# Squares streamed past a column of ones, and small operations on VectorE ahead of the steps

## The reference, cut to what matters

```
xn = layer_norm(logmap0(x));  xm = expmap0(xn * (1 + sc) + sh)
q, k, v = heads of expmap0(logmap0(xm) @ w + b)          # 16 heads of 16 numbers
out_h = expmap0(softmax(qt kt / 4) vt);  attn_out = expmap0(logmap0(out_h) @ w_o + b_o)
x = mobius_add(x, expmap0(g * logmap0(attn_out)))
ff = expmap0(logmap0(expmap0(logmap0(xm') @ w_f1 + b_f1)) @ w_f2 + b_f2)
x = mobius_add(x, expmap0(g' * logmap0(ff)))
```

```
a = x_t @ Wx + h @ Wh + b;  i, f, o = sigmoid(...);  g = tanh(...)
c = f * c + i * g;  h = o * tanh(c)
```

## Time and profile before

| | us |
|---|---|
| median of 3 runs | 1776.1 |
| lowest and highest run | 1774.89, 1791.21 |
| profiled execution, its own time | 1775.52 |
| span of the profile | 1773.8 |

### The profile page before, as it was taken

One profiled execution on the slowest core, in us unless ns is written; L12 is line 12 of the kernel. 1 busy time (PEld: TensorE's weight loads), 2 busy tenths in 40 slices (PEclk: granted clock), 3 DMA queues, 4 the chain that ended last, 5 costly groups with the idle time before them and its releaser, 6 DMA issues.

```text
span 1773.8 us, 59205 instructions
## 1 busy us (share of the span) xinstructions
PE 1325.2 (75%) x22039; PEld 1125.0 (63%) x22039; DVE 1168.5 (66%) x6498; ACT 940.3 (53%) x3335; POOL 520.5 (29%) x1438
## 2 busy tenths in 40 slices
PE   3656568758569797978888888988696877868654
PEld 3544455536458686867777777867575766757543
DVE  6465566654376777777677777676666666666665
ACT  0333458766346565666666665655454454545433
POOL 4122213365441324242332414142313214040100
PEclk9676765555656565656566665556565565656555
DMA  7000000000000000000000000000000000000000
GB/s 237 0 0 0 0 1 1 2 1 1 4 3 9 3 9 2 9 3 8 3 9 3 9 3 9 2 9 8 3 9 2 9 2 9 3 5 5 3 5 5
DMA packets 16685, 17.97 MB, mean 10 GB/s; under 512 B 6036, under 2 KB 15384, under 8 KB 16408
## 3 DMA queue, kind: packets, MB, share of 16 engines
q1 hardware_dynamic: 13016, 10.51, 2.1%
q10 hardware_dynamic: 3392, 3.81, 0.8%
HBM read 12.21 MB, written 2.10 MB: 8 GB/s over the span
## 4 chain that ended last, share of the span: by engine, by line
PE 49%; DVE 17%; ACT 5%; issue 4%; POOL 2%; DVEq 0%; POOLq 0%
PE psum L741 27%; PE psum L717 5%; PE psum L692 4%; DVE cnew L1227 4%; ACT ot L964 4%; PE psum L685 4%; DVE hl L1236 4%; DVE hl L1234 3%; DVE gO L1222 3%; PE psum L731 3%; PE psum L620 2%; DVE cadd L1224 2%; PE psum L700 1%; PE psum L667 1%; PE psum L632 1%
## 5 line engine op out<-in xcount | busy, mean ns | idle before, releaser
L741 PEld LDWEIGHTS psum<-hl,wh 128*128 128x128 f16 x16384 | 496.7, 103 | 352.9 <-DVE hl L1236 331.7
L741 PE MATMUL psum<-hl,wh 128*128 128x8 f16 x16384 | 524.0, 172 | 259.8 <-DVE hl L1236 259.0
L958 ACT ACTIVATE tA<-gA 128x16 f32<-128x16 f32 x512 | 110.4, 216 | 465.5 <-DVE gA L1218 465.5
L1218 DVE TENSOR_REDUCE gA<-psum 128x16 f32<-128x32 f32 x512 | 97.2, 190 | 216.1 <-PE psum L741 213.1
L1112 DVE TENSOR_TENSOR weights<-w,weights 128x256 f16<-128x256 f32 x512 | 202.8, 419 | 35.2 <-ACT weights L861 34.2
L867 ACT ACTIVATE w<-psum 128x512 f32<-128x512 f32 x256 | 156.2, 610 | 24.7 <-DVE weights L1112 22.8
L861 ACT ACTIVATE weights<-psum 128x512 f16<-128x512 f32 x256 | 155.3, 607 | 8.3 <-PE psum L632 8.1
L620 PE MATMUL psum<-qTs,kT 64*128 64x128 f16 x1024 | 146.6, 293 | 16.8 <-ACT weights L861 13.8
L256 POOL TENSOR_TENSOR sc<-sc,cst 128x1 f32<-128x1 f32 (+1 forms) x180 | 148.2, 823 | 33.8 <-POOL sc L304 12.2
L1234 DVE TENSOR_TENSOR hl<-ot 128x8 f16<-128x8 f32 x512 | 89.9, 176 | 91.2 <-ACT ot L964 89.3
L964 ACT ACTIVATE ot<-cnew 128x8 f32<-128x8 f32 x512 | 109.4, 214 | 72.7 <-DVE cnew L1227 12.7
(11 more groups left out here) (244 smaller groups left out, 2434.4 us busy)
## 6 DMA issues: line engine op xcount, KB each, us to landing
arena<-in_x_dram SPq DMA_DIRECT2D x4, 512.0 KB, 9.7
wf<-in_L_cond_w_f_dram SPq DMA_DIRECT2D x2, 1024.0 KB, 16.7
xr<-in_x_dram SPq DMA_DIRECT2D x64, 32.0 KB, 1.7
out_dram<-place SPq DMA_DIRECT2D x64, 32.0 KB, 1.6
qTs<-in_L_cond_w_ada_dram ACTq DMA_DIRECT2D x1, 1536.0 KB
oT<-in_L_cond_Wh_dram ACTq DMA_DIRECT2D x1, 1024.0 KB, 14.3
wx<-in_L_cond_Wx_dram SPq DMA_DIRECT2D x1, 1024.0 KB, 18.6
rows<-in_L_cond_b_ada_dram ACTq DMA_DIRECT2D x4, 128.0 KB, 14.0
```

The lines of the kernel that those rows point to most:

```text
L741: last = mm(cols, wh16[:, half, kc, (g0 + c) * P:(g0 + c + 1) * P], hl[:, :, kc, :, 2].rearrange("p e b -> p b e"), start=False, stop=c == ...
```

## The change

- The squares: the column of ones is now the stationary operand and each chunk of squares the moving one, 128 columns long. The sum comes out as one row of 128 numbers in a single partition. VectorE copies that row to SBUF at r=41 (`nfrow`), TensorE turns it by a product with a single one at r=42, and VectorE copies the column at r=42. GpSimd's (or VectorE's) clip moves from r=42 to r=43.
- Ahead of the steps (merges 0 to 7, tile 0, tile 1 up to r=32) VectorE does the small operations. GpSimd does only the powers with exponent 0.5 and -0.5: VectorE raises `q_in` (`ask`) and waits for `q_out` before it goes on. Reciprocals, which were powers with exponent -1, are VectorE's own there. From slot 0 on, GpSimd does all of it as before.
- One of the eight pairs of the first feed-forward matrix moves from r=31 to r=32.
- `keep_busy` loses its branch for the slots ahead; its constants stay 0.

```diff
-WF1_AT = (26, 27, 28, 29, 30, 31, 33, 34)
+WF1_AT = (26, 27, 28, 29, 30, 32, 33, 34)
...
-WANTED, EARLY, FIRST_STEPS = 0, 0, 0
+WANTED, FIRST_STEPS = 0, 0
...
+def ahead(n, r):
+
+    return RING * n - PAUSE + r < 0
...
+            def powers(*those):
+
+                nonlocal asked
+                asked += 1
+                hold(pool, "q_in", asked)
+                for dst, src, which, w in those:
+                    last = g.tensor_tensor(dst, src, cst[:, which, 0:w], ALU.pow)
+                last.then_inc(s["q_out"], 1)
+
             def merged(k, r):
...
+                if k < 2 * B:
+                    if r == 2:
+                        powers((num("rh", H), num("smx", H), HALF_DOWN, H))
+                    if r == 4:
+                        powers((one("cbm"), one("cam"), HALF_DOWN, 1))
+                    return
...
                     for c in (2 * (r - 38), 2 * (r - 38) + 1):
-                        last = mm(pM[:, 0:1], fsq[:, c, :], ones[:, 0:1], start=c == 0, stop=c == KF - 1, skip_group_check=True)
+                        last = mm(pM[0:1, 0:P], ones[:, 0:1], fsq[:, c, :], start=c == 0, stop=c == KF - 1, skip_group_check=True)
                     if r == 41:
                         last.then_inc(s["n_nf"], 1)
+                if r == 42:
+                    pe.wait_ge(s["n_nfr"], n + 1)
+                    mm(pM[:, D:D + 1], nfrow[0:1, :], ones[0:1, 0:1], start=True, stop=True, skip_group_check=True).then_inc(s["n_nft"], 1)
...
+            def ask(last):
+
+                nonlocal asked
+                asked += 1
+                last.then_inc(s["q_in"], 1)
+                v.wait_ge(s["q_out"], asked)
+
+            def merged_ahead(k, r):
...
+                    link(d.tensor_tensor(num("rd2", H), F("rd"), F("rd"), ALU.mult))
+                    link(d.tensor_tensor(num("ssn", H), num("ssh", H), num("rd2", H), ALU.mult))
+                    d.tensor_scalar(num("smn", H), num("ssn", H), REACH * REACH, None, ALU.min).then_inc(s["m_mn"], 1)
+                    ask(d.tensor_scalar(num("smx", H), num("ssn", H), 1.0, None, ALU.max))
+                    link(d.tensor_scalar(num("fr", H), num("rh", H), REACH, 1.0, ALU.mult, ALU.min))
+                    link(d.tensor_tensor(num("fd", H), num("fr", H), F("rd"), ALU.mult))
...
+                    ask(d.tensor_scalar(one("cam"), one("now"), 1.0 / (HEAD * HEAD), TINY, ALU.mult, ALU.max))
+                    link(d.tensor_scalar(one("sow"), one("cbm"), REACH, 1.0, ALU.mult, ALU.min))
+                    d.tensor_scalar(num("F", H), num("fd", H), one("sow"), 1.0 / HEAD, ALU.mult, ALU.mult).then_inc(s["m_F"], 1)
...
+            def post_ahead(n, r):
+
+                if r == 5:
+                    v.wait_ge(s["n_n1"], n + 1)
+                    v.wait_ge(s["n_n2"], n + 1)
+                    rows_arg("A", "n_ar")
...
             def post(n, r):
 
+                if ahead(n, r):
+                    post_ahead(n, r)
...
                 if r == 41:
                     v.wait_ge(s["n_nf"], n + 1)
-                    d.tensor_copy(one("nfn"), pM[:, 0:1]).then_inc(s["n_nfc"], 1)
+                    d.tensor_copy(nfrow[0:1, :], pM[0:1, 0:P]).then_inc(s["n_nfr"], 1)
+                if r == 42:
+                    v.wait_ge(s["n_nft"], n + 1)
+                    d.tensor_copy(one("nfn"), pM[:, D:D + 1]).then_inc(s["n_nfc"], 1)
```

More of the change, by code:

```diff
@@ L161, in bass_hyperbolic_block_then_lstm @@
         mv1 = sb("mv1", [P, 2])
+        nfrow = sb("nfrow", [1, P])
         c0T = sb("c0T", [P, KD, B])
@@ L492, in mobius_factors @@
                 g.tensor_scalar(N("be"), N("fac"), N("nb"), N("den"), ALU.mult, ALU.mult).then_inc(s[done], 1)
+            def post_ahead(n, r):
+                if r in (5, 48):
+                    p = "A" if r == 5 else "B"
+                    powers((one("cb" + p), one("ca" + p), HALF_DOWN, 1), (one("n2i" + p), one("cd" + p), HALF_DOWN, 1))
+                if r == 12:
+                    powers((one("ta"), one(f"x2q{n % 2}"), HALF_UP, 1))
+                if r == 17:
+                    powers((one("ta"), one("tc"), HALF_DOWN, 1))
+                if r == 23:
+                    powers((one("cbu"), one("cau"), HALF_DOWN, 1))
+                if r == 43:
+                    powers((one("cbf"), one("caf"), HALF_DOWN, 1))
             def post(n, r):
+                if ahead(n, r):
+                    post_ahead(n, r)
+                    return
                 if r == 5:
@@ L519, in post @@
                     clip(ch, one("sun"), one("nun"), 1, one("cau"), one("cbu"), s["n_su"])
-                if r == 42:
+                if r == 43:
                     hold(pool, "n_nfc", n + 1)
@@ L778, in keep_busy @@
                 cols, us = beside(t)
-                if t >= 0:
-                    count = int(min((WANTED - 256 - cols) / D, (1.2 - us) * 2400 / D))
-                    if t < 4:
-                        count = (FIRST_STEPS - 256 - cols) // D
-                else:
-                    count = (EARLY - cols) // D if t in HEAD_AT else 0
-                if count > 0 and t >= 0:
+                count = int(min((WANTED - 256 - cols) / D, (1.3 - us) * 2400 / D))
+                if t < 4:
+                    count = (FIRST_STEPS - 256 - cols) // D
+                if count > 0:
                     pe.wait_ge(s["l_gF"], t + 1)
@@ L793, in _ @@
                 pieces(t, attention, merged, post, out_rows)
-                if t < T - 1:
+                if 0 <= t < T - 1:
                     keep_busy(t)
@@ L1142, in merged @@
                     d.tensor_reduce(one("now"), num("smn", H), axis=AX.X, op=ALU.add).then_inc(s["m_now"], 1)
+                if k < 2 * B:
+                    merged_ahead(k, r)
                 if r == 7:
@@ L1148, in merged, with rows_clip, rows_arg @@
                                     ALU.mult).then_inc(s["m_oS"], 1)
+            def rows_clip(dst, nsq, a, b, done):
+                ask(d.tensor_scalar(a, nsq, TINY, None, ALU.max))
+                d.tensor_scalar(dst, b, REACH, 1.0, ALU.mult, ALU.min).then_inc(s[done], 1)
+            def rows_arg(p, done):
+                N = lambda name: one(name + p)
+                d.tensor_scalar(N("ca"), N("n1"), TINY, None, ALU.max)
+                ask(d.tensor_scalar(N("cd"), N("n2"), TINY, None, ALU.max))
+                link(d.tensor_scalar(N("s1"), N("cb"), REACH, 1.0, ALU.mult, ALU.min))
+                d.tensor_scalar(N("ar"), N("cd"), N("n2i"), N("s1"), ALU.mult, ALU.mult).then_inc(s[done], 1)
@@ new lines, in rows_factors @@
+            def rows_factors(p, nsq_x, done):
+                N = lambda name: one(name + p)
+                d.tensor_scalar(N("nb"), nsq_x, -1.0, 1.0, ALU.mult, ALU.add)
+                d.tensor_tensor(N("y2"), N("th"), N("th"), ALU.mult)
+                link(d.tensor_tensor(N("fac"), N("th"), N("n2i"), ALU.mult))
+                link(d.tensor_scalar(N("xy"), N("xa"), 2.0, N("fac"), ALU.mult, ALU.mult))
+                d.tensor_scalar(N("cu"), N("y2"), 1.0, N("xy"), ALU.add, ALU.add)
+                link(d.tensor_scalar(N("cv"), N("y2"), nsq_x, N("xy"), ALU.mult, ALU.add))
+                link(d.tensor_scalar(N("cw"), N("cv"), 1.0, EPS, ALU.add, ALU.max))
+                link(d.reciprocal(N("den"), N("cw")))
+                d.tensor_tensor(N("al"), N("cu"), N("den"), ALU.mult).then_inc(s[done], 1)
+                d.tensor_scalar(N("be"), N("fac"), N("nb"), N("den"), ALU.mult, ALU.mult).then_inc(s[done], 1)
```

69 lines of the change are left out of this document (66 added, 3 removed).

## The result

The changed kernel takes 1802.9 us (median of 13 runs, 1799.0 to 1812.0) against 1790.8 of the kernel before in the same comparison (13 runs, 1773.2 to 1804.9). The ratio is **1.0138, 95% interval 1.0107 to 1.0168**: slower. It leaves out runs over 1.5% above the fastest of their kernel, here two of the kernel before and none of the changed one; with all 26 runs the means stand at 1.010, slower too. The profiled execution took 1799.0 us, its span is 23.5 us longer than before's.

The account below looks back on a forecast made before the run. Steps were taken as bound by the recurrence, or TensorE where its pieces don't fit; ahead, by ScalarE, TensorE and GpSimd's tail in turn. Terms 4.3 + 1 - 3.4 + 4.5 + 1 = +7.4 gave 1783 us, range 1764 to 1802.

Parts of the forecast that it names:

- VectorE ahead: Ahead of the steps, small operations on VectorE, GpSimd keeping powers: stage terms of +4.3, +1 and -3.4 us, others 0.
- Merges 0 to 2: Slots to 331.7 us: VectorE's stop moves to r=2, 4.1 us felt per merge against 2.65: +4.3 us (0 to +9.8).
- The stretch behind them: From 331.7 to 396.8 us: VectorE becomes the bound, 62.7 of 65.1 us busy: +1 us (-3 to +7).
- The rest: From 396.8 us to the first step: 0 where TensorE is full, -3.4 in the tail, 0 beside the gates.
- Squares: Slots of the squares in the steps: streaming 128 columns stays under the slot's 2.33 us, so 0 us.
- The turn: One more product at r=42, where TensorE is full: 0.3 us in each of 15 tiles, +4.5 us (3.7 to 7.4).
- Clock rises lost: Just after r=43: added loads stretch the products ahead, so some clock rises won't come: +1 us (0 to 3).
- The pair: Feed-forward pair moved from r=31 to r=32: r=31 shorter, r=32 longer, set at 0 us (-3 to +6).
- streaming: Rival: streamed squares keep the clock up through r=38 to 43, giving 1758 to 1771 us; chance 0.10.
- VectorE in series: Rival, ahead of the steps: each VectorE stop reaches ScalarE whole; with 5.5 in the steps, 1802 us; chance 0.17.
- the case of idle time: Rival: VectorE's stops ahead fall into idle time: -8, -2.4 and -6, with +4.5 in the steps, 1764 us; chance 0.13.
- The signs: Wrong if clock up at r=42, first 64 units over 82 or under 73 us, or steps without these pieces change.

Follow-up runs that it names:

- the run without a turn: Kernel before with streamed squares but no turn product at r=42, the factor taken from a constant; GpSimd ahead, pair at r=31: ratio 1.0053.
- the two executions of VectorE ahead: Kernel before with only the small operations ahead of the steps moved to VectorE, profiled twice: spans 1794.4 and 1777.7 us; timed ratio 1.0003.

## Why the prediction was wrong

The forecast was 1783 us in a range up to 1802, with "the same" (within one per cent) at 0.72; the kernel takes 1802.9 and is slower by 1.4%. The forecast was added to a median of three runs, 1776.1, of a kernel whose runs reach 1804.9.

- *VectorE ahead.* Close, with the other sign: +1.9 forecast, -1.8 in the profile, -3.6 and -2.6 when done alone. Merges 0 to 2: +5.3 (forecast +4.3). The stop moved to r=2 as said, 3.5 felt against 4.1, but this makes only 2.3 of the 5.3; 2.9 are ScalarE's waits for TensorE's scores, which the prediction didn't have. That the sum came near is partly luck. The stretch behind them: -3.3 (forecast +1, bounds -3 to +7, so just outside). There the sum took VectorE for the bound with 62.7 of 65.1, waits for GpSimd in it; the measured stretch is 61.8, shorter than that demand, so the prices were too high there. No run takes that stretch apart. The rest: -3.9 (forecast -3.4). The price of the way back, 0.2, was too high for a power of 16 columns: 0.04.
- *Squares.* Nearly right for their own slots: without attention these stay at 2.33, and TensorE spends 64.4 us on the products against 63.0; the cost is not 0 but 1.9 us, all with attention beside them (1.5 in the run without a turn). What the sum didn't have is the rest of the +10.9 us of that run, in other steps.

```profile
L740 PE MATMUL psum<-arena,ones 128*1 128x128 f32 x256 | 64.4, 405 | 0.7 <-ACT arena L973 0.7
L745 PE MATMUL psum<-ones,nfrow 1*128 1x1 f32 x32 | 9.3, 358 | 0.3 <-DVE nfrow L1349 0.3
```

- *The turn: the step that failed.* The prediction said that it is on the path in all 15 tiles, which is right, and priced it at 0.3 "nearer the lower end", because "its first load can run under the product ahead". The first load of a one-row stationary operand doesn't, here: 0.63, outside the bounds (0.25 to 0.49), +9.4 us and not +4.5. With 128 rows the same product costs 0.24 when nobody reads it and 0.30 as a turn, and the reasoning holds. So the size came from a row of other shape: all products of the earlier trace rows had 128 rows.
The Trainium skill (TensorE: Matmul & The Clock Gate, section "Step-by-step: what each phase is for") says that TensorE pulls a load ahead of running products where the row groups don't conflict or the load goes to the background buffer. For 128 rows this case's trace agrees (0.63 ahead). For one row behind a product of 128 rows the load isn't pulled ahead (it starts 0.07 before that product's end); the trace doesn't show which of the two conditions fails there.
- *Clock rises lost: the second step that failed.* +1 was forecast, 0 to 3, and only for the rise just after r=43. For that place the term was right: r=43 and r=44 take 2.0 us more, and the rise is gone there as said. But all that isn't r=42 comes to 15.5 us. Most of it shows up half a tile away, at r=28 to r=32, where 4.75 and 3.68 stand against each other for the same instructions. The experiments show that a product at r=42 brings a loss beyond its own step without any other edit (1.0105 with 0.20% of direct cost), that the streamed squares alone do so too (1.0053), and that VectorE ahead can have it or not in two executions of one program.
- *The pair.* Forecast 0: r=31 shorter and r=32 longer, as said, and neutral or a small gain (0.9966 alone). The price of r=32 with attention at half clock is the dear one, 4.24, against 3.38 for the same step before:

```profile
1159.70:1163.94 4.24, 4.24 (x48) 3.78 (x47) 1.79 (x11) 2.15 (x7) 0.00 (x0) 0.50 0.02 4
```
- *Rivals.* The clock isn't up at r=42 (0.50), so streaming doesn't keep it up. VectorE in series gave the right total, 1802, for a wrong reason: ahead of the steps nothing was lost. Behind merge 2 the stages came near the case of idle time (-3.3 and -3.9 against its -2.4 and -6), merges 0 to 2 did not (+5.3 against its -8).
- *The signs.* Of those that the prediction named against itself one came true: steps without any of the pieces changed (r=28 to 30). r=42 at 3.37 instead of 3.05 was the first to see.

What stays open: what decides in which steps the clock is up. Profiles with a product of 0.24 us had longer steps (1320.7 and 1324.9) than those with one of 0.63 us (1307.6 and 1308.0), and streamed squares alone had 1304.4. The mean clock doesn't tell it either: in the comparison with the squares' part alone, the runs of the kernel before with a mean clock of 0.590 took 1783.9 to 1786.5 us, those of the squares' part with 0.589 or 0.590 took 1800.3 to 1801.9. That is some 16 us at the same mean clock, of which r=42 is 9.4. The profiles show where the clock was up, not why the two levels were granted there; so this part of the loss is located, and its cause isn't shown.

## What to carry to other kernels

Price an added product from a row of the same shape, rows of the stationary operand included: ask for each load whether it starts before the product ahead ends. In a kernel whose clock moves between its levels, an edit in a slot where TensorE is full can cost more than what it adds, in steps far from it; here that was more than the edit itself. So put added TensorE work where there is room (at r=45 the profile's steps stayed as they were), and judge it by many runs, since one profile shows only one of the ways in which the clock can rise and fall.

## What the runs showed of the hardware

- A float32 load of one row takes about as long as one of 128 rows. The lines of the turn in the two forms (all 32 instructions: duration ns least/median/greatest), one row and then 128:

```profile
L745 PEld LDWEIGHTS psum<-ones,nfrow x32: 283/308/333, 432.4 to 1662.7; 1*128 1x128 f32 x32
  issue: 9.8, 15
```
```profile
L745 PEld LDWEIGHTS psum<-ones,nfrow x32: 288/337/338, 429.4 to 1648.1; 128*128 128x128 f32 x32
```

The second line of the first is the load queue's idle time ahead of the one-row loads: 9.8 us in 15 places, 0.65 each; the form with 128 rows has none. Columns do count: the column of ones, now the stationary operand of the squares, is one column of 128 rows, and its loads are four times shorter.

```profile
L740 PEld LDWEIGHTS psum<-arena,ones x256: 79/83/128, 422.0 to 1658.7; 128*1 128x1 f32 x128
```

The Trainium skill (the same page, section "LDWEIGHTS (loading the stationary operand)") says that a load's time goes by its columns and not by its rows; on the rows the trace agrees, while the 107 ns that its formula gives for 128 columns are a third of what one of the two float32 loads of the turn takes here (308 ns).
- In the longer of the two executions of VectorE ahead, steps at half clock are each longer by 0.5 to 0.7% than in the other, with the same instructions: those in which TensorE is full (r=42 of one tile below, the longer, then the shorter execution), and also those of r=37 without attention, 2.346 against 2.333 us. Over 1300 us that would be up to 6 to 9 us (an estimate from these steps), so not all of the 17.7 between them need be the clock's levels; no run here shows where it comes from.

```profile
1342.63:1345.40 2.77, 2.77 (x37) 2.20 (x38) 1.88 (x13) 0.84 (x4) 1.05 (x3) 0.50 0.00 0
```
```profile
1327.68:1330.43 2.75, 2.75 (x37) 2.17 (x38) 1.84 (x13) 0.83 (x4) 1.05 (x3) 0.50 0.00 0
```
